# Seven written-out passes of a fused attention kernel turned into a hardware loop

## The chip, the cores and the metric

The kernel runs on one core of a Trainium2 chip. The metric is the device time of one execution in microseconds (us). TensorE multiplies matrices, VectorE (DVE), ScalarE (ACT) and GpSimd (POOL) do the elementwise work, and SyncE (SP) starts the loads and stores. Each engine has a sequencer that reads the engine's instructions one after another.

## The reference

Four blocks run one after another on `x` of shape (32, 128, 128): 32 sequences of 128 tokens with 128 features. Cut down:

```
x = L0(x, ctx, mask)    # self-attention and cross-attention, 16 heads of 64, each with
                        # a residual and a layer norm; then a ReLU MLP 128-512-128, the same
x = L1(x, ctx, skip)    # attention, 16 heads of 8, ReLU on q, k, v; + x
x = L2(x, ctx)          # an encoder layer on ctx + ctx, then a decoder layer with two
                        # linear attentions (elu + 1), 8 heads of 16, layer norms, ReLU MLPs
r = x + mha(norm(x), norm(ctx))                 # L3: 8 heads of 16
U = (norm(r) @ W_in.T + b_in) @ Bmat            # (32, 128, 64)
s_t = silu(s_(t-1) @ A.T) + U_t                 # 128 steps in order
out = r + states @ Cmat + mod                   # mod: one row for each sequence
```

Everything is float32, except for the masks inside the kernel. All but the recurrence over `t` treats the 32 sequences apart from one another.

## The kernel before

The 32 sequences go in 8 groups of 4 (`GROUPS`, `G`), so a tile has 128 partitions and 4 x 128 = 512 columns. The work on a group falls into two streams. The main stream is L0. The side stream is L1, L2 and L3 up to `U`. A pass `g` does the main stream of group `g` together with the side stream of group `g - 1`. So the kernel has these stages: pass 0 (main stream of group 0 with the setup of the weights), passes 1 to 7 (main and side), the side stream of group 7 alone, the scan over 128 steps, and the final sum with the stores.

Each compute engine has its own program for the two streams, as Python generators `main(i)` and `side(i)`, and `interleave` merges them step by step by the list `SIDE_PACE`; the order of each engine's instructions is thus fixed when the program is built. `main_fills` and `side_fills` give the order in which PSUM banks are filled, and who empties them (A for ScalarE, D for VectorE). The engines go in step by semaphores that only count up: `filled` by TensorE, `emptied` by ScalarE and VectorE, and some twenty more. A wait names the value that its semaphore must have reached, and that value is worked out from the pass: `Pass.at(each, n)` gives `g * each + n`, where `each` is how often the semaphore is raised in one pass and `n` the place in it.

All eight passes are Python loops over `g`, so their instructions are written out eight times with constant wait values. The scan and the final sum at the end are different: there `Fori`, a hardware loop with a counter in a register on each engine, holds the steps (16 scan steps in each round), with wait values and some addresses worked out from the counter.

At the end of a pass ("seam" below) TensorE turns the last normalised tile, VectorE empties it into `xT["b"]` and hands over to the side stream in `hand_over` (L1255, L1256, L1258: `x_side`, `c_side` and the mask `attend`, then `handed` goes up). The program of TensorE ends a pass with a wait for that emptying:

```python
elif kind == "n":
    before_filling(i, item, (tag, "y"))
    turn4(MAIN, item, lambda b: main_normed[:, b, :])
    if tag == "ln3":
        wait_emptied(pe, i, MAIN, item)
```

The next pass begins on TensorE with the turn of `x_in` (L642) and the side stream's products (L646), on VectorE with the masks (L1189 to L1195). SyncE has its own Python loop over the groups and starts the loads of group `g` when pass `g - 1` has read its inputs.

Of the kernel before, what the change touches and what calls it, by code (L numbers as in the profile page):

```python
# [32 lines left out]
GROUPS = B // G  # L33
# [61 lines left out]
SIDE_STEPS = len(SIDE_PACE)  # L95
SETUP_STEPS = 9


class Stream:


    def __init__(self, fills):
        self.order = [name for name, _, _ in fills]
        self.fill = {name: n + 1 for n, name in enumerate(self.order)}
        self.bank = {name: bank for name, bank, _ in fills}
        self.by = {name: by for name, _, by in fills}
        self.total = {"A": 0, "D": 0}
        self.rank = {}
        for name, _, by in fills:
            self.total[by] += 1  # L110
            self.rank[name] = self.total[by]
        self.fills = len(fills)

        self.before, last = {}, {}
        for name, bank, _ in fills:
            self.before[name] = last.get(bank)
            last[bank] = name


def main_fills():  # L120

    order, n = [], 0
    for item in (x for step in MAIN_STEPS for x in step if x[1] not in NO_FILL):
        tag, kind = item[:2]
        if kind == "s":
            bank = item[2] % 2
        elif kind == "o":
            bank = 3
        elif kind == "y":
            bank = 0  # L130
        elif item[:3] == ("ca", "v", 1) and item[3] < 2:
            bank = (1, 3)[item[3]]
        else:
            bank, n = (2, 4)[n % 2], n + 1
        if kind in ("v", "y", "n"):
            by = "D"
        elif kind in ("k", "o") or tag in ("ffn", "in"):
            by = "AD"[item[-1] % 2]
        else:
            by = "A"  # L140
        order.append((item, bank, by))
    return order
# [34 lines left out]
MAIN, SIDE = Stream(main_fills()), Stream(side_fills())  # L177
# [43 lines left out]
class Pass:  # L221


    def __init__(self, g):
        self.g = g

    def at(self, each, n):
        return self.g * each + n


def interleave(main, side, pace=SIDE_PACE):

    taken, due = 0, 0
    for n, _ in enumerate(main):
        while side is not None and taken < len(pace) and due * len(MAIN_STEPS) < (n + 1) * sum(pace):
            next(side)
            due += pace[taken]
            taken += 1
    assert side is None or next(side, "end") == "end"


def alone(stream):

    return sum(1 for _ in stream)


def build_program(nc, I, out):
    with ExitStack() as ctx:
# [149 lines left out]
        def wait_filled(eng, i, st, name):  # L398

            eng.wait_ge(filled[st], i.at(st.fills, st.fill[name]))  # L400

        def wait_emptied(eng, i, st, name):

            by = st.by[name]
            eng.wait_ge(emptied[st, by], i.at(st.total[by], st.rank[name]))
# [16 lines left out]

        def passes(eng, main, side, setup):

            interleave(main(Pass(0)), setup, [1] * SETUP_STEPS)
            for g in range(1, GROUPS):
                interleave(main(Pass(g)), side(Pass(g - 1)))
            assert alone(side(Pass(GROUPS - 1))) == SIDE_STEPS

        n_first, n_ca, n_rest, n_const = [0], [0], [0], [0]  # L430

# [2 lines left out]
        def _(sp):  # L434
# [4 lines left out]
            def load_inputs(g):  # L439
                for dst, name in ((x_in, "x"), (c_in, "ctx_1024")):  # L440
                    sp.dma_start(dst[:, :, :], I[name][g * G:g * G + G, :, :].rearrange("g t e -> t g e")).then_inc(group_in, 16)

            def load_valid(g):
                m = I["mask_BxS2_bf1"].rearrange("b t -> (b t)")[g * GT:g * GT + GT].partition_broadcast(128)
                sp.dma_start(valid_in[:, :], m).then_inc(group_in, 16)

            def load_skip(g):
                m = I["mask_BxS_ik0"].rearrange("b t -> (b t)")[g * GT:g * GT + GT].partition_broadcast(128)
                sp.dma_start(skip_in[:, :], m).then_inc(skip_loaded, 16)
# [27 lines left out]
            load_skip(0)  # L477
            for g in range(1, GROUPS):

                wait_filled(sp, Pass(g - 1), MAIN, ("in", 1))  # L480
                load_inputs(g)
                sp.wait_ge(masks_taken, g)
                load_valid(g)
                sp.wait_ge(handed, g)
                load_skip(g)
# [9 lines left out]
        def _(pool):  # L495
# [61 lines left out]
            def side(i):  # L557
# [69 lines left out]
                yield  # L627

            passes(pool, main, side, None)


        @block.tensor
        def _(pe):
# [61 lines left out]
            def turn(i, item):  # L695
                tag, _, u = item
                before_filling(i, item)
                pe.wait_ge(scaled, i.at(2 * UNITS, u + 1 + (0 if tag == "sa" else UNITS)))
                for h in range(4):
                    last = nc.tensor.transpose(bank(MAIN, item)[:, h * 128:h * 128 + 128],  # L700
                                               probs[:, u % 3, h * 128:h * 128 + 128], ident[:, :])
                last.then_inc(filled[MAIN], 1)
# [202 lines left out]
            def setup_side():  # L905
# [19 lines left out]
                yield  # L925

            passes(pe, main, side, setup_side())


# [33 lines left out]
        def _(act):  # L963
# [62 lines left out]
            def side(i):  # L1026
# [44 lines left out]
                yield  # L1071

            passes(act, main, side, None)

            def scan_step(t, k):
# [13 lines left out]
        def _(dve):  # L1089
            V = nc.vector  # L1090
            count = {setup_step: 0, main_step: 0, side_step: 0}
            each = {setup_step: SETUP_VSTEPS, main_step: MAIN_VSTEPS, side_step: SIDE_VSTEPS}

            def link(i, s, ins):

                count[s] += 1
                ins.then_inc(s, 1)
                dve.wait_ge(s, i.at(each[s], count[s]))

            once = Pass(0)  # L1100
            dve.wait_ge(consts_ready, n_const[0])
            link(once, setup_step, V.tensor_copy(ident_h[:, :], ident[:, :]))
            link(once, setup_step, V.tensor_copy(causal[:, :], main_normed[:, 0, :]))
# [148 lines left out]
            def hand_over(i):  # L1252

                wait_emptied(dve, i, MAIN, ("ln3", "n"))
                V.tensor_scalar(x_side[:, :], xT["b"][:, :], 1.0, None, ALU.mult)  # L1255
                V.tensor_scalar(c_side[:, :], cT[:, :], 1.0, None, ALU.mult)  # L1256
                dve.wait_ge(skip_loaded, i.at(16, 16))
                V.tensor_scalar(attend[:, :], skip_in[:, :], 0.0, D1 ** -0.5, ALU.not_equal, ALU.mult).then_inc(handed, 1)  # L1258
# [25 lines left out]
            def side(i):  # L1284
# [85 lines left out]
                yield  # L1370

                def group(n):
                    return slice(i.g * n, i.g * n + n)
                link(i, side_step, V.tensor_tensor(x2_all[:, group(GT)].rearrange("p (g t) -> p g t", g=G),
                                                   x1T[:, :].rearrange("p (g t) -> p g t", g=G),
                                                   mod[:, group(G)].unsqueeze(2).broadcast_to([128, G, T]), ALU.add))
# [6 lines left out]

            interleave(main(once), setup_side(), [1] * SETUP_STEPS)
            hand_over(once)
            for g in range(1, GROUPS):
                interleave(main(Pass(g)), side(Pass(g - 1)))
                hand_over(Pass(g))
            assert alone(side(Pass(GROUPS - 1))) == SIDE_STEPS

            dve.wait_ge(emptied[SIDE, "D"], GROUPS * SIDE.total["D"])

# [41 lines left out]
```

## Time and profile before

| | |
|---|---|
| median of 3 runs | 2718.73 us (2716.09 to 2722.7) |
| the profiled execution | 2722.7 us, span 2721.0 us |
| instructions recorded | 32500 |
| passes 1 to 7 (239.4 to 2306.0 us) | 2066.6 us |
| mean granted clock of TensorE | 0.903 |
| instruction fetch | two queues, 1.43 MB and 0.54 MB |

Times come from one execution by the hardware profiler, except for the first line. "Busy" counts neither waits nor the register, branch and semaphore instructions of the sequencers. The granted clock of TensorE is 1.00 at 2.4 GHz and 0.50 at 1.2 GHz. In a row of the timeline the bracket at the end is how long the engine had stood idle before it, and whose work released it. A pass is read here from one hand-over (L1255) to the next.

### The profile page before, as it was taken

What the parts mean: (1) busy time and instruction counts of PE and PEld (TensorE: products, weight loads), DVE (VectorE), ACT (ScalarE), POOL (GpSimd) and SP (SyncE); (2) the same over time, 40 slices, a digit from 0 to 9 for tenths busy, and PEclk for the clock granted to TensorE, in tenths of its full rate; (3) what the DMA queues carried; (4) which work ended last, traced back from release to release, by engine and by line L of the source; (5) the groups of instructions that cost most, each with busy time, mean ns of one, the idle gap of its engine ahead of it and who ended that gap; (6) DMA issues with size and microseconds to landing.
All of it is one profiled execution on the core that took longest, in us unless ns stands there. A gap on an engine that the chain in (4) does not pass through costs nothing.

```text
span 2721.0 us, 32500 instructions
## 1 busy us (share of the span) xinstructions
PE 2321.0 (85%) x11161; PEld 1613.0 (59%) x11161; DVE 1502.9 (55%) x3998; ACT 1168.8 (43%) x4001; POOL 340.7 (13%) x349
## 2 busy tenths in 40 slices
PE   5887988898888988898889888998889888865898
PEld 3555655666565665565556656566556555543596
DVE  4554666565756666566656674666656665233212
ACT  3452635364544645363536454454536353210221
POOL 0002011101112011201110111101120121012000
PEclk9988999999999999999999998999999999566555
DMA  5000000000000000000000000000000000000001
GB/s 152 1 1 13 1 1 1 13 2 1 1 1 13 1 1 1 13 1 1 1 13 1 1 1 1 13 1 1 1 5 1 1 1 1 0 0 0 1 0 31
DMA packets 24511, 19.75 MB, mean 7 GB/s; under 512 B 1699, under 2 KB 22182, under 8 KB 24358
## 3 DMA queue, kind: packets, MB, share of 16 engines
q1 hardware_dynamic: 24358, 17.78, 2.3%
q8 instruction: 87, 1.43, 0.2%
q14 instruction: 66, 0.54, 0.1%
HBM read 15.68 MB, written 2.10 MB: 7 GB/s over the span
## 4 chain that ended last, share of the span: by engine, by line
PE 65%; DVE 21%; ACT 7%; issue 4%; POOL 3%; SPq 0%; DMA 0%; POOLq 0%; DVEq 0%
PE ps L646 13%; PE ps L654 8%; PE ps L787 7%; PE ps L689 7%; PE ps L712 6%; PE ps L770 4%; PE ps L780 4%; DVE tok L1158 3%; PE ps L700 3%; ACT probs L977 3%; DVE keys L1225 2%; PE ps L939 2%; PE ps L642 2%; DVE stats L1145 2%; POOL kx L563 2%
## 5 line engine op out<-in xcount | busy, mean ns | idle before, releaser
L977 ACT ACTIVATE probs<-ps,neg_max 128x128 f32<-128x128 f32 x1024 | 361.8, 366 | 419.4 <-DVE neg_max L1138 412.6
L977 ACT ACTIVATE s_probs<-ps,s_max 128x128 f32<-128x128 f32 x768 | 218.8, 367 | 274.0 <-DVE s_max L1138 273.9
L689 PE MATMUL ps<-keys,queries 128*128 128x256 f32 x1024 | 281.3, 398 | 28.4 <-ACT queries L971 28.4
L712 PE MATMUL ps<-probsT,values 128*128 128x256 f32 x1024 | 277.8, 395 | 3.7 <-ACT headsT L1011 2.7
L787 PE MATMUL ps<-kx,qT 32*128 32x512 f32 (+1 forms) x384 | 244.5, 720 | 33.5 <-POOL kx L563 33.5
L1138 DVE TENSOR_REDUCE neg_max<-ps 128x4 f32<-128x512 f32 x256 | 176.4, 689 | 162.7 <-PE ps L692 161.4
L1138 DVE TENSOR_REDUCE s_max<-ps 128x4 f32<-128x512 f32 x192 | 132.5, 690 | 235.7 <-PE ps L787 233.5
L689 PEld LDWEIGHTS ps<-keys,queries 128*128 128x128 f32 x1024 | 187.4, 195 | 119.6 <-ACT queries L971 42.4
L540 POOL TENSOR_TENSOR rstd<-var_eps,minus_half 128x4 f32<-128x4 f32 x88 | 90.3, 1026 | 1235.3 <-DVE var_eps L1151 1234.6
L1145 DVE BATCH_NORM_STATS2 stats<-ps 128x6 f32<-128x128 f32 x352 | 78.2, 284 | 299.4 <-PE ps L654 295.6
L712 PEld LDWEIGHTS ps<-probsT,values 128*128 128x128 f32 x1024 | 178.8, 194 | 67.3 <-issue 25.1
L977 ACT ACTIVATION_READ_ACCUMULATOR probs<-ps,neg_max 128x1 f32 x1024 | 208.7, 204 | 0.0
L700 PEld LDWEIGHTS ps<-ident,probs 128*128 128x128 f32 x1024 | 123.5, 142 | 128.2 <-issue 81.9
L971 ACT ACTIVATE probsT<-ps 128x512 f32<-128x512 f32 x256 | 155.7, 608 | 50.7 <-PE ps L700 49.5
L770 PEld LDWEIGHTS ps<-l1v,s_probsT 128*128 128x128 f32 x1024 | 143.9, 209 | 51.9 <-issue 49.3
L700 PE MATMUL ps<-ident,probs 128*128 128x128 f32 x1024 | 158.6, 278 | 0.4 <-DVE probs L1181 0.4
L642 PE MATMUL ps<-ident,tok 128*128 128x128 f32 x352 | 61.6, 302 | 103.8 <-DVE tok L1158 89.6
L646 PE MATMUL ps<-xT_a,w_qkv_sa 128*128 128x512 f32 x256 | 132.1, 603 | 12.8 <-DVE cT L1210 11.0
L780 PE MATMUL ps<-ident,s_probs 128*128 128x128 f32 x768 | 133.0, 300 | 10.3 <-ACT s_probs L977 7.3
L534 POOL TENSOR_TENSOR pool_scratch<-minus_half 128x1 f32<-128x1 f32 x88 | 17.0, 193 | 985.0 <-DVE x1T L1275 672.1
L770 PE MATMUL ps<-l1v,s_probsT 128*128 128x9 f32 x1024 | 137.1, 261 | 0.7 <-ACT s_probsT L971 0.7
L1240 DVE COPY headsT<-ps 64x256 f32<-64x256 f32 x256 | 107.5, 420 | 40.3 <-PE ps L712 38.2
(211 smaller groups left out, 4088.9 us busy)
## 6 DMA issues: line engine op xcount, KB each, us to landing
x_in<-in_x SPq DMA_DIRECT2D x8, 256.0 KB, 3.0
c_in<-in_ctx SPq DMA_DIRECT2D x8, 256.0 KB, 3.3
skip_in<-in_mask_BxS_ik SPq DMA_DIRECT2D x8, 256.0 KB, 3.1
out<-x_all SPq DMA_DIRECT2D x8, 256.0 KB, 2.3
valid_in<-in_mask_BxS_bf SPq DMA_DIRECT2D x8, 64.0 KB, 3.4
w_qkv_sa<-in_L_xattn_sa_wq SPq DMA_DIRECT2D x1, 512.0 KB
w_qkv_sa<-in_L_xattn_sa_wk SPq DMA_DIRECT2D x1, 512.0 KB
w_qkv_sa<-in_L_xattn_sa_wv SPq DMA_DIRECT2D x1, 512.0 KB
```

The lines of the kernel that those rows point to most:

```text
L646: mm(bank(st, name)[0:lhs.shape[-1], :], lhs, rhs, start=True, stop=True).then_inc(filled[st], 1)
L654: last = mm(dst, l, r, start=(n == 0), stop=(n == len(todo) - 1))
L689: mm(bank(MAIN, item)[:, n * 256:n * 256 + 256], queries[:, c % 2, at], keys[:, c % 2, :, at], start=(n == 0), stop=False, skip_group_chec ...
L700: last = nc.tensor.transpose(bank(MAIN, item)[:, h * 128:h * 128 + 128], probs[:, u % 3, h * 128:h * 128 + 128], ident[:, :])
L712: last = mm(bank(MAIN, item)[:, n * 256:n * 256 + 256], values[:, c // 4, b0 + n, (c % 4) * 128:(c % 4) * 128 + 128], probsT[:, u % 2, n * ...
L770: last = mm(bank(SIDE, (tag, "o", b))[:, at:at + d1], s_probsT[:, u % 2, h * 128:h * 128 + 128], value[:, b, q * 4 + h, :], start=True, st ...
L780: last = nc.tensor.transpose(bank(SIDE, (tag, "t", u))[:, h * 128:h * 128 + 128], s_probs[:, u % 2, h * 128:h * 128 + 128], ident[:, :])
L787: mm(bank(SIDE, (tag, "s", s)), qT[part, b * T:b * T + T], kx[part, :, b * T:b * T + T], start=True, stop=True).then_inc(filled[SIDE], 1)
L971: A(dst, view(s) if view else s, fn, **kw).then_inc(emptied[st, "A"], 1)
L977: last = A(dst[:, u % dst.shape[1], h * 128:h * 128 + 128], bank(st, (tag, "s", u))[:, h * 128:h * 128 + 128], ACT.Exp, bias=src_max[:, u ...
L1138: V.tensor_reduce(dst[:, u % 2, :], bank(st, (tag, "s", u)).rearrange("p (h k) -> p h k", h=4), AX.X, ALU.max, negate=True).then_inc(max_r ...
L1145: last = V.bn_stats(stats[:, slot, b, :], bank(st, (tag, "y"))[:, b * 128:b * 128 + 128])
```

## The change

The passes 1 to 7 become one hardware loop of 7 rounds on TensorE, ScalarE, VectorE and GpSimd. `Pass` now holds an optional register `r` and a constant offset: in a round, the main stream is `Pass(r, 1)` and the side stream `Pass(r, 0)`, and a wait value is `r * each + (offset * each + n)`. Pass 0 and the last side stream keep constants. On VectorE `hand_over` is in the loop, and two instructions at the end of the side stream take their addresses in `x2_all`, `mod` and `u_all` from the register (`bass.ds`). SyncE keeps its written-out list.

```diff
-    def __init__(self, g):
-        self.g = g
+    def __init__(self, r, offset):
+        self.r, self.offset = r, offset
 
     def at(self, each, n):
-        return self.g * each + n
+        known = self.offset * each + n
+        return known if self.r is None else self.r * each + known
...
-            interleave(main(Pass(0)), setup, [1] * SETUP_STEPS)
-            for g in range(1, GROUPS):
-                interleave(main(Pass(g)), side(Pass(g - 1)))
-            assert alone(side(Pass(GROUPS - 1))) == SIDE_STEPS
+            interleave(main(Pass(None, 0)), setup, [1] * SETUP_STEPS)
+            with eng.Fori(0, GROUPS - 1) as r:
+                interleave(main(Pass(r, 1)), side(Pass(r, 0)))
+            assert alone(side(Pass(None, GROUPS - 1))) == SIDE_STEPS
...
-                wait_filled(sp, Pass(g - 1), MAIN, ("in", 1))
+                wait_filled(sp, Pass(None, g - 1), MAIN, ("in", 1))
...
                 def group(n):
-                    return slice(i.g * n, i.g * n + n)
+                    return slice(i.offset * n, i.offset * n + n) if i.r is None else bass.ds(i.r * n + i.offset * n, n)
...
-            for g in range(1, GROUPS):
-                interleave(main(Pass(g)), side(Pass(g - 1)))
-                hand_over(Pass(g))
-            assert alone(side(Pass(GROUPS - 1))) == SIDE_STEPS
+            with dve.Fori(0, GROUPS - 1) as r:
+                interleave(main(Pass(r, 1)), side(Pass(r, 0)))
+                hand_over(Pass(r, 1))
+            assert alone(side(Pass(None, GROUPS - 1))) == SIDE_STEPS
```

## Rows read from the trace of the kernel before

**Rows 1.** The page: busy time by engine; granted clock in 40 slices.
```profile
PE 2321.0 (85%) x11161; PEld 1613.0 (59%) x11161; DVE 1502.9 (55%) x3998; ACT 1168.8 (43%) x4001; POOL 340.7 (13%) x349
...
PEclk9988999999999999999999998999999999566555
```

**Rows 2.** Windows by stage: stretch, length, busy by engine (instructions), PEclk, DMA, GB/s.
```profile
239.40:2306.00 2066.60, 1814.13 (x9212) 1247.50 (x9212) 1277.89 (x3353) 998.10 (x3388) 293.96 (x287) 0.97 0.01 3
2306.00:2572.00 266.00, 192.42 (x592) 120.59 (x592) 79.28 (x234) 48.69 (x130) 33.70 (x32) 0.57 0.00 0
```

**Rows 3.** Windows of single passes, the longest and the shortest, same columns.
```profile
534.40:831.50 297.10, 261.37 (x1317) 179.24 (x1317) 182.42 (x480) 142.58 (x484) 41.89 (x41) 0.96 0.01 4
...
1125.00:1418.50 293.50, 257.29 (x1316) 177.25 (x1316) 182.74 (x479) 142.59 (x484) 42.13 (x41) 0.98 0.01 4
```

**Rows 4.** The page: chain that ended last, by engine.
```profile
PE 65%; DVE 21%; ACT 7%; issue 4%; POOL 3%; SPq 0%; DMA 0%; POOLq 0%; DVEq 0%
```

**Rows 5.** Timeline at one seam: start, us, engine, line, op, operands, count, idle before.
```profile
1122.84 0.63 PE L642 MATMUL ps<-ident,main_normed 128*128 128x128 f32 x4 [1.47 <-DVE main_normed L1158]
1123.33 1.00 DVE L1377 TENSOR_SCALAR u_all<-ps 64x512 f32<-64x512 f32 x1
1124.19 0.77 DVE L1171 TENSOR_SCALAR xT_b<-ps,col_all 128x512 f32<-128x512 f32 x1
...
1125.02 0.66 PE L642 MATMUL ps<-ident,x_in 128*128 128x128 f32 x4 [1.55 <-DVE xT_b L1171]
...
1125.68 0.42 DVE L1258 TENSOR_SCALAR qT<-skip_in 128x512 f32<-128x512 int32 x1
1125.71 0.60 ACT L971 ACTIVATE xT_a<-ps 128x512 f32<-128x512 f32 x1 [5.47 <-PE ps L642]
...
1126.15 1.12 PE L646 MATMUL ps<-x_side,turned 128*128 128x512 f32 x2 [0.47 <-DVE qT L1258]
```

**Rows 6.** Windows of 3.4 us at that seam.
```profile
1120.40:1123.80 3.40, 1.60 (x6) 0.51 (x6) 2.43 (x6) 0.00 (x0) 0.90 (x1) 1.00 0.00 0
1123.80:1127.20 3.40, 1.71 (x7) 0.99 (x8) 3.30 (x8) 0.60 (x1) 0.81 (x2) 0.99 0.01 4
1127.20:1130.60 3.40, 3.40 (x12) 2.37 (x11) 2.53 (x5) 0.69 (x1) 3.40 (x4) 0.50 0.21 73
```

**Rows 7.** DMA view: instruction queue (packets, MB, share); loads, KB each, us to landing.
```profile
q8 instruction: 87, 1.43, 0.2%
...
valid_in<-in_mask_BxS_bf SPq DMA_DIRECT2D x8, 64.0 KB, 3.4
...
kx<-in_L_xattn_W_prog SPq DMA_DIRECT2D x1, 32.0 KB, 1.9
```

**Rows 8.** Waits of TensorE: total us, times, longest.
```profile
PE ps L689 <- ACT queries L971: 28.4, 32, 2.5
```

**Rows 9.** Timeline of the scan, ScalarE, then VectorE.
```profile
2573.49 0.19 ACT L1079 ACTIVATE state<-ps 64x32 f32<-64x32 f32 x1 [2.56 <-PE ps L935]
...
2586.28 0.19 ACT L1079 ACTIVATE state<-ps 64x32 f32<-64x32 f32 x1 [0.72 <-PE ps L939]
2587.28 0.19 ACT L1079 ACTIVATE state<-ps 64x32 f32<-64x32 f32 x1 [0.81 <-PE ps L939]
2588.27 0.19 ACT L1079 ACTIVATE state<-ps 64x32 f32<-64x32 f32 x1 [0.80 <-PE ps L939]
2589.18 0.19 ACT L1079 ACTIVATE state<-ps 64x32 f32<-64x32 f32 x1 [0.72 <-PE ps L939]
...
2602.08 0.19 ACT L1079 ACTIVATE state<-ps 64x32 f32<-64x32 f32 x1 [0.83 <-PE ps L939]
...
2586.28 0.18 DVE L1397 TENSOR_TENSOR u_all<-u_all,state 64x32 f32<-64x32 f32 x1 [0.73 <-PE ps L939]
...
2589.29 0.18 DVE L1397 TENSOR_TENSOR u_all<-u_all,state 64x32 f32 x1 [0.80 <-PE ps L939]
```

**Rows 10.** The page: the turn of `probs` on TensorE; last columns are idle before.
```profile
L700 PE MATMUL ps<-ident,probs 128*128 128x128 f32 x1024 | 158.6, 278 | 0.4 <-DVE probs L1181 0.4
```

More of the change, by code:

```diff
@@ L1098, in link @@
                 dve.wait_ge(s, i.at(each[s], count[s]))
-            once = Pass(0)
+            once = Pass(None, 0)
             dve.wait_ge(consts_ready, n_const[0])
```

## The prediction

> **What bounds the kernel now.** I read the page first. One core is busy 85% of the span on TensorE, 55% on VectorE, 43% on ScalarE and 13% on GpSimd [rows 1]; no engine is full, so the order of the work decides. Next, the stages: passes 1 to 7 take 2066.6 of 2721.0 us, and the last side stream alone 266.0 [rows 2]. The change acts on passes 1 to 7 only. Pass by pass they take 293.5 to 297.1 us, and the longer ones have the lower mean granted clock, 0.96 against 0.98 [rows 3]. The chain of waits is 65% TensorE, 21% VectorE, 7% ScalarE and 4% "issue" [rows 4]: within a pass the queue of TensorE sets the pace, with short stops for VectorE and ScalarE. Then I read one seam between two passes in time [rows 5]. TensorE turns `main_normed` at 1122.84, VectorE empties that bank by 1124.96, and at 1125.02 TensorE turns `x_in` for the next pass. VectorE meanwhile hands over until 1126.10, and TensorE starts the side stream's first product at 1126.15. So TensorE is already thinly used here, and the clock is granted at half for the 3.4 us that follow [rows 6].
>
> **The change, part by part.** The work, its tiles, semaphores, counts and order stay. What goes is the written-out code of six of the seven middle passes on TensorE, ScalarE, VectorE and GpSimd. What comes is (a) a jump back after each of the first six rounds, (b) arithmetic for every wait value inside the round, since `Pass.at` now holds a register, and (c) register addresses for two VectorE instructions per pass. SyncE keeps its written-out list, so loads and their order do not move. Pass 0 and the side stream after the loop keep constant waits.
>
> (a) **The jump.** A loop is already in this kernel: the scan, 7 rounds of 16 steps. Written-out steps follow one another in 0.913 us (2573.49 to 2586.28 is 14 steps), so 16 of them would take 14.62; a round takes 14.80 (2587.28 to 2602.08) [rows 9]. Jump and register work together cost 0.2 us per round. That body is short. The body here is long: instruction fetches come in packets of 16 KB on one queue, 87 packets in the execution [rows 7], which is 1.43 MB, over ten packets for each of the eight passes. I take it that such a body is no longer at hand when the jump asks for its head, and that the first packet has to be fetched while the engine stands. The trace of before has no such stop. From below it is 0.2 us (the scan's round); from above it is a transfer that nobody prepared. Loads take 1.9 us from issue to landing for 32 KB and 3.4 us for the 64 KB of `valid_in` [rows 7]. I take 3.0 us, near the upper of these rows because a sequencer that has run dry also has to ask for the packet, and 0.2 for the jump itself: 3.2 us.
>
> Whom does it stop? TensorE's last act in a pass is to wait for VectorE's emptying of `("ln3","n")`; the jump stands behind that wait, so its fetch begins at about 1125.0 and nothing of TensorE's covers it. Of that time TensorE would in any case stand 0.47 us before 1126.15, waiting for the hand-over [rows 5], so 3.2 - 0.5 = 2.7 us are exposed. ScalarE has nothing to do for the 5.47 us before 1125.71 [rows 5], so its own fetch is covered. VectorE's sequencer is ahead of its engine: with waits riding on queued instructions it reaches the jump about when `u_all` begins (1123.3) and has its packet by about 1126.5, 0.4 us after the hand-over ends; its masks are then 0.4 us late, under TensorE's 2.7. GpSimd has 41 instructions in a pass [rows 3] and waits most of it. So the four jumps overlap and TensorE's counts: 6 x 2.7 = 16 us. If TensorE's fetch were covered too, the term would be 6 x 0.2 = 1 us; if VectorE's whole 3.2 stood behind them, 6 x 5.9 = 35 us.
>
> The Trainium skill, "Runtime: NRT & Kernel Launch", section "Instruction fetch mechanics", says that fetching is sequential and mostly hidden, and that a taken branch to a target outside the fetched window stalls for the fetch, which would make the term the 16 us above and not 1; the rows of before neither show nor exclude that stall. The skill's "Advanced Engine Details and Errata", section "Control Flow Timing", gives 108 ns for a compare-and-branch; six of them would be an estimate of 0.6 us, against 0.2 us per round in the scan, which holds register work as well.
>
> **The clock.** At the seam TensorE is busy 1.60 and 1.71 of 3.4 us in two stretches and then gets the half clock for one such stretch, 1127.2 to 1130.6 [rows 6]. With 2.7 more idle microseconds I expect the low stretch to be one stretch longer. The price of low clock comes from rows 3: 297.1 us at 0.96 against 293.5 at 0.98 is 3.6 us for a low share greater by 4 points of 295, or 12 us: 0.3 us per us. One stretch costs 3.4 x 0.3 = 1.0 us; at most, with TensorE never waiting, 1.7. Six: 6 us, between 0 and 10.
>
> (b) **Register waits.** Per pass the code has some 366 waits on TensorE, 312 on VectorE, 168 on ScalarE and 26 on GpSimd (counted in the program). Each value now takes an addition by the sequencer. In the scan the same forms cost nothing in 14 of 16 steps: ScalarE starts 0.72 us after its release in both kinds of code. In the first two steps of a round it starts 0.81 and 0.80 after [rows 9]; there the addition for a second wait carries the first wait, so that the sequencer stands where before the queued instruction stood. That is 0.09 us per such stop. On VectorE the step with a register address starts at 2589.29 where ScalarE's starts at 2589.18, 0.11 us later, while both start at 2586.28 in written-out code. TensorE has some 118 places per pass with two waits or more. Written out, the second wait was an instruction of its own and the first rode on the work; in the loop this turns round. Where the last release is the first wait of the code, the place loses 0.09 us; where it is the second, it gains. TensorE stood 32 times for `queries` in the execution, 4 times in a pass [rows 8], at `scores`, where the first wait is the one released last: 4 x 0.09 x 7 = 2.5 us, which I round to 3; the other places I take as even. Elsewhere the additions run ahead of the array, which is busy 0.6 to 1 us per group while an addition is a matter of the sequencer alone. If that cover is gone, all 118 lose: 118 x 7 x 0.09 = 74 us. If all gain, it is -74.
>
> (c) **Register addresses.** Two VectorE instructions per pass, late by 0.11 us each, at the end of the side stream: 1.5 us over seven, of which I count none. The bound is 1.5, since they stand right ahead of VectorE's last work at the seam.
>
> **Sum** against the profiled execution: 2722.7 us (span 2721.0), plus 16 (jumps), 6 (clock), 3 (waits): 2747.7. The median of the runs shown is 2718.7, 4.0 below that execution, so I predict 2744 us, 0.9% more.
>
> **Rivals.**
> - **Cheap jump.** The head of the body is there when wanted, as in the scan, or the fetch is covered by the seam's idle time. Then 6 x 0.2 + 3 = 4 us: 2722, within measuring error. For it: TensorE idles 1.8 of its 3.4 us at the seam already, and the scan. Against: a body of ten packets, and a last wait that holds TensorE's jump until 1125.0, after which only 0.47 us of its time is free.
> - **Dear waits.** The additions hold the TensorE sequencer in many places, and it loses its lead over the array. 40 to 74 us on top of the jumps: about 2780 to 2815. For it: 118 double waits in a pass and "issue" already 4% of the chain. Against: 14 of 16 steps of the scan.
> - **Turned waits gain (the other sign).** Most TensorE stops come from the wait that now rides on the work itself. It is faster than before by more than 0.2% only if more than 25 + 5.4 = 30 us are won, over 340 of the 826 places at 0.09 us, or with cheap jumps over 70 net. At two thirds of the places net: 2744 - 3 - 50 = 2691. Against: the clearest place of that kind, the turn of `probs` with `scaled` as its second wait, held the array idle for 0.4 us in the whole execution [rows 10].
>
> **How the numbers follow.** Forecast 0.68; its own range is 2731 (fetch 1.9 us, so 1.6 exposed, and no clock term: 10 + 3 us over the median) to 2767 (35 + 10 + 3 us over it). Cheap jump 0.14. Dear waits 0.12. Turned waits 0.06. About 0.2%, 5.4 us, is what a measurement of this kernel can tell from no change. Cheap jump gives 0.12 same and 0.02 slower: faster 0.06, same 0.12, slower 0.82. The range 2721 to 2785 leaves out the gaining case, most of the dear waits and a sliver of the cheap jumps, just under 0.2 together.
>
> **What the profile after would show.** Passes 2 to 7, each entered by a jump, are 3 to 5 us longer; pass 1, entered by falling through, is not, and neither are the side stream alone, the scan or pass 0. The gap before TensorE's turn of `x_in` grows from 1.5 to about 4.7 us at six seams, with the releaser no longer VectorE's; the half clock behind it lasts about 6.8 us. Busy times stay. If instead all seven passes are longer, by gaps spread over the attention, it is the waits. If no seam widens, the jump is cheap. What would make me wrong: a fetch of several microseconds that also repeats inside the body, a stall on VectorE that outlasts TensorE's, or clock stretches elsewhere in the pass that shift by chance.

## The result, and the profile after

The changed kernel takes 2753.4 us (median of 4 runs, 2748.5 to 2757.3) against 2717.5 for the kernel before: a ratio of 1.0129, 95% interval 1.011 to 1.0148, or 36 us more. The forecast was 2744 us, 25 more than the 2718.7 known then. The profiled execution took 2753.06 us, its span is 2751.3. Some executions of these kernels run slower throughout at a lower granted clock, and every ratio here leaves them out.

The page of the changed kernel, busy time and granted clock:

```profile
PE 2333.3 (85%) x11161; PEld 1616.3 (59%) x11161; DVE 1504.4 (55%) x3998; ACT 1170.6 (43%) x4001; POOL 340.6 (12%) x349
...
PEclk9998999999999999999999999999999999566555
```

The counts of [rows 1] have not changed. TensorE is busy 12 us longer on the same 11161 products, at a mean granted clock of 0.895 in place of 0.903; VectorE and ScalarE are busy less than 2 us longer. Below are the windows of single passes (stretch, length, busy time of each engine with its instructions, granted clock, DMA share, GB/s). A pass runs from one handing over of `x_side` to the next, and the first shown is pass 1:

```profile
241.91:537.49 295.58, 260.87 (x1316) 179.06 (x1316) 182.31 (x480) 142.87 (x484) 41.96 (x41) 0.96 0.01 4
537.49:837.37 299.88, 259.73 (x1316) 177.87 (x1316) 182.85 (x479) 142.85 (x484) 41.96 (x41) 0.96 0.01 4
...
1137.84:1438.20 300.36, 261.47 (x1316) 179.48 (x1316) 182.81 (x480) 142.74 (x484) 41.95 (x41) 0.95 0.01 4
...
2038.94:2339.34 300.40, 261.42 (x1316) 179.54 (x1316) 182.82 (x480) 142.73 (x484) 41.96 (x41) 0.95 0.01 2
```

Pass 1, entered by falling through, is 0.6 us longer than in the first trace of before; the six passes entered by a jump are 2.8 to 6.9 us longer than the same passes there, 30.2 in sum. The two spans differ by 30.3: the passes behind a jump account for it. Pass 0 is 2.5 us longer and the part behind pass 7 is 3.0 us shorter, which nearly cancel. Against passes of 293.5 us [rows 3] each of them is 6.4 to 7.0 us longer.

One seam in time (start, us, engine, line, operation, operands, idle before and what ended it). It answers to [rows 5]:

```profile
1437.39 0.77 DVE L1172 TENSOR_SCALAR xT_b<-ps,col_all 128x512 f32<-128x512 f32 x1
1438.20 0.43 DVE L1256 TENSOR_SCALAR x_side<-xT_b 128x512 f32<-128x512 f32 x1
...
1441.61 0.43 DVE L1190 TENSOR_SCALAR mask_ca<-valid_in 128x512 bf16<-128x512 uint8 x1 [2.31 <-issue]
...
1442.51 1.11 PE L643 MATMUL ps<-ident,x_in 128*128 128x128 f32 x4 [6.08 <-issue]
...
1443.42 1.92 PE L647 MATMUL ps<-x_side,turned 128*128 128x512 f32 x2
```

VectorE has emptied `xT_b` at 1438.16. Before, TensorE turned `x_in` 0.06 us later; now 4.35 us later, and the releaser is no longer VectorE but "issue". This is the longest of the six: counted from the start of the hand-over, the turn comes 3.75 to 4.31 us later, 4.0 in the mean, where it was 0.02. The view of waits has this stop six times, once a seam; below it is the wait at `scores` that answers to [rows 8]:

```profile
PE ps L643 <- issue: 34.7, 6, 6.1
...
PE ps L690 <- ACT queries L972: 29.3, 32, 2.3
```

The second has grown by 0.9 us in all. The first is not spread over the loop's code: one instruction has it, the branch. Six of them take 3.40 to 3.96 us; the seventh, at 76 ns, falls out of the loop. The view of the loop's line, TensorE's sequencer (count, then min/median/max in ns):

```profile
L427 PEldq COMPARE_BRANCH  x7: 76/3618/3958, 537.7 to 2339.5; - x7
```

The queue of instruction packets, in the DMA view, against 87 packets and 1.43 MB in [rows 7] (the second such queue goes from 0.54 to 0.93 MB):

```profile
q8 instruction: 108, 1.77, 0.3%
```

VectorE's `mask_ca` is 2.31 us late too, by its own jump, but that ends ahead of TensorE's. Last, the clock. Rows of 3.4 us at the seam before that one, against one such row at half clock in [rows 6], and then six further rows of the same pass, the first of them at full clock:

```profile
1136.70:1140.10 3.40, 0.00 (x0) 0.00 (x0) 2.21 (x5) 0.00 (x0) 0.00 (x0) 0.50 0.05 14
1140.10:1143.50 3.40, 1.91 (x6) 1.40 (x7) 2.39 (x5) 0.60 (x1) 0.08 (x1) 0.50 0.23 77
1143.50:1146.90 3.40, 3.40 (x9) 1.85 (x8) 0.92 (x2) 0.69 (x1) 3.40 (x5) 0.50 0.00 0
1259.60:1263.00 3.40, 1.38 (x7) 0.86 (x8) 3.35 (x9) 0.00 (x0) 0.18 (x1) 1.00 0.01 2
1263.00:1266.40 3.40, 3.40 (x9) 1.85 (x8) 0.80 (x2) 1.19 (x2) 1.74 (x2) 0.50 0.00 0
1283.50:1286.90 3.40, 3.40 (x8) 1.80 (x8) 1.80 (x3) 0.00 (x0) 1.68 (x2) 0.51 0.00 0
1355.10:1358.50 3.40, 3.16 (x10) 2.04 (x10) 2.75 (x6) 2.98 (x11) 0.00 (x0) 0.50 0.02 5
1368.80:1372.20 3.40, 3.40 (x9) 2.28 (x8) 0.55 (x2) 1.77 (x6) 0.00 (x0) 0.50 0.00 0
1420.00:1423.40 3.40, 3.14 (x7) 1.32 (x5) 2.52 (x11) 0.48 (x1) 2.46 (x3) 0.50 0.00 0
```

In this pass the granted clock is half (1.2 of 2.4 GHz) for 27.3 us, eight rows' worth, and 10.2 us of that lie together at the seam. A pass of 293.5 us of the first trace has 13.7 us, four rows' worth. Passes 2 to 7 have 18.0 us in the mean in the first trace of before and 25.8 here.

### The profile page after: what moved, and what is told of

It is laid out like the page before. It is cut to its first block, busy times and chain, and to the rows that moved or that the text cites. A ratio compares the mean times of both kernels' runs of the same rounds, so it can differ in the third digit from the quotient of the medians.

```text
span 2751.3 us, 37417 instructions
## 1 busy us (share of the span) xinstructions
PE 2333.3 (85%) x11161; PEld 1616.3 (59%) x11161; DVE 1504.4 (55%) x3998; ACT 1170.6 (43%) x4001; POOL 340.6 (12%) x349
## 4 chain that ended last, share of the span: by engine, by line
issue 69%; PE 13%; POOL 11%; DVE 4%; ACT 2%; SPq 0%; POOLq 0%; DMA 0%; DVEq 0%
POOL kx L564 4%; POOL rstd L541 3%; PE ps L940 2%; PE ps L647 2%; PE ps L936 2%; POOL s_probsT L569 2%; POOL main_residual L554 1%; PE ps L788 1%; PE ps L655 1%; ACT probs L978 1%; PE ps L690 1%; ACT s_probs L978 1%; PE ps L781 1%; PE ps L953 1%; POOL pool_scratch L535 1%
## 5 line engine op out<-in xcount | busy, mean ns | idle before, releaser
L535 POOL TENSOR_TENSOR pool_scratch<-minus_half 128x1 f32<-128x1 f32 x88 | 17.1, 195 | 1015.2 <-DVE x1T L1276 670.9
```

## The experiments

Each ratio is against the kernel before on the same chip. Its median was 2709.4 us next to the first four kernels below (registers, the two split loops, two passes to a round), 2710.4 next to the hint, the moved wait, the pause of eight copies and the lighter seam, and 2714.2 next to the last four (the pause of two copies, before again, registers on TensorE, hint with lighter seam).

**Registers without a jump.** The kernel before, written out; on all four engines every wait value and address of the middle passes comes from a register that holds 0.

```diff
+            zero = nc.alloc_registers("base", engines=[eng.engine])
+            nc.regs_mov(zero, 0)
+            r = nc.snap(zero, min_val=0, max_val=1)
             for g in range(1, GROUPS):
-                interleave(main(Pass(g)), side(Pass(g - 1)))
+                interleave(main(Pass(r, g)), side(Pass(r, g - 1)))
```

> The seven passes are written out as before, but every wait value and the two VectorE addresses are worked out from a register that holds 0, as in the loop: the arithmetic without the jump. Theory (the jump stops TensorE at six seams, and the rest is small): 0 to +5 us over before, as pass 1 of the changed kernel, entered without a jump, is only 0.6 us longer than before (295.6 against 295.0). Rival (dear waits): +20 to +36 us, the whole of the change's cost, and the passes grow by gaps inside the attention.

Measured 2725.8 us, ratio 1.006 (1.0043 to 1.0076): 16 us, not 0 to 5. The gaps in the attention have not grown. The weight loads of the turn of `probs`, whose second wait is `scaled`, on the page of this kernel:

```profile
L704 PEld LDWEIGHTS ps<-ident,probs 128*128 128x128 f32 x1024 | 125.3, 144 | 128.3 <-issue 122.2
```

Its idle time is 128.3 us; in before the same group of weight loads has 128.2, with another releaser named for a part of it. Its execution in the trace is the fastest of its six, 2722.5 us. Three of its passes are as short as before's shortest (windows, the first and a long one):

```profile
537.55:831.06 293.51, 257.39 (x1316) 176.97 (x1316) 182.69 (x480) 142.87 (x484) 42.15 (x41) 0.98 0.01 4
...
1124.33:1421.23 296.90, 261.67 (x1316) 179.50 (x1316) 182.78 (x480) 142.74 (x484) 41.96 (x41) 0.96 0.01 4
```

So the registers don't lengthen a pass evenly; they make more passes long. What has grown is the gap at the seam (timeline, hand-over at 1421.23):

```profile
1419.56 1.00 DVE L1381 TENSOR_SCALAR u_all<-ps 64x512 f32 x1 [0.21 <-DVE x_all L1378]
...
1421.41 1.11 PE L646 MATMUL ps<-ident,x_in 128*128 128x128 f32 x4 [1.96 <-DVE xT_b L1175]
```

TensorE stands 1.96 us ahead of `x_in` at each of these six seams, in place of 1.55. VectorE's instruction with a register address waits 0.21 us right ahead of the emptying, and the turn itself starts 0.18 us after the hand-over begins in place of 0.02.

The chain on the page of the changed kernel has 69% "issue" against 4% in [rows 4]. Here, with no jump and 16 us lost, it has 66%, so that share does not measure what the jump costs.

**Only TensorE loops; all but TensorE loop; two passes to a round.** In the first, ScalarE, VectorE and GpSimd are written out with constants, in the second TensorE is; the third has three rounds of two passes and pass 7 written out, so two jumps in place of six. The upper part of the diff is of the first (only TensorE's stream has a `setup` here; the second turns the condition round), the lower of the third.

```diff
+            if setup is not None:
+                with eng.Fori(0, GROUPS - 1) as r:
+                    interleave(main(Pass(r, 1)), side(Pass(r, 0)))
+            else:
+                for g in range(1, GROUPS):
+                    interleave(main(Pass(None, g)), side(Pass(None, g - 1)))
...
+            with eng.Fori(0, 3) as q:
+                for n in range(2):
+                    interleave(main(Pass(q * 2, n + 1)), side(Pass(q * 2, n)))
+            interleave(main(Pass(None, 7)), side(Pass(None, 6)))
```

> TensorE alone loops; ScalarE, VectorE and GpSimd have written-out passes with constants. Theory: nearly the whole cost, +28 to +36 us over before, since TensorE's branch takes 3.4 to 4.0 us at each of six seams and the half clock behind it lasts 10.2 us instead of 3.4. Rival (the stops of several engines add up): clearly less, +10 to +22 us, with the rest in the run without TensorE's loop.

> ScalarE, VectorE and GpSimd loop as in the changed kernel; TensorE's seven passes are written out with constants. Theory (TensorE's jump counts, the other engines' jumps lie under it): TensorE's 4.4 us stop at six seams goes; what is left is VectorE's jump, which in the changed kernel ends 2.3 us after its hand-over, so +1 to +2.5 us for each of six seams plus a little clock: +6 to +18 us over before. Rival (VectorE's jump sets the seam just as well, both stand side by side): +25 to +36 us. Rival (only TensorE's jump costs): 0 to +4 us.

> Three rounds of two passes each, pass 7 written out: two jumps instead of six, register values in six passes instead of seven. Theory (5.0 us for each jump): 2 x 5 = 10 us over before, +8 to +14 with the waits' small share; of the passes only those entered by a jump (the third and the fifth) grow. Rival (dear waits): about as slow as the changed kernel, +28 us or more. Rival (a long body costs more as it gets longer, by fetches inside it): the passes not entered by a jump grow too.

TensorE alone: 2746.9 us, ratio 1.0135 (1.0117 to 1.0152), as much as the whole change. The other three alone: 2731.5, ratio 1.0075 (1.0059 to 1.0091), 22 us where 6 to 18 were expected, and 6 above the registers alone. Two jumps: 2736.4, ratio 1.0094 (1.0076 to 1.0111), 27 us where 8 to 14 were expected: that one missed, by about what the registers cost. With the other engines' loop the passes have one length (windows; the other five behind a jump lie between 296.96 and 297.11):

```profile
829.38:1126.36 296.98, 260.15 (x1316) 177.79 (x1316) 183.50 (x480) 142.57 (x484) 42.08 (x41) 0.97 0.01 4
```

At its seam TensorE goes on at once, and VectorE's stop of 2.01 us lies under its work (timeline, hand-over at 1126.36):

```profile
1126.38 1.12 PE L647 MATMUL ps<-ident,x_in 128*128 128x128 f32 x4 [1.73 <-DVE xT_b L1176]
...
1129.47 0.75 DVE L1194 TENSOR_SCALAR mask_ca<-valid_in 128x512 bf16<-128x512 uint8 x1 [2.01 <-issue]
```

In the kernel with two jumps, exactly the two passes behind a jump are at 300.4 us:

```profile
827.04:1127.41 300.37, 261.49 (x1316) 179.42 (x1316) 183.14 (x480) 142.74 (x484) 41.95 (x41) 0.95 0.01 4
1127.41:1424.38 296.97, 261.69 (x1316) 179.47 (x1316) 182.78 (x479) 142.73 (x484) 41.96 (x41) 0.96 0.01 4
1424.38:1724.78 300.40, 261.38 (x1316) 179.55 (x1316) 182.80 (x479) 142.72 (x484) 41.99 (x41) 0.95 0.01 4
```

**The jump with a hint.** The changed kernel, each engine's stream told of the jump's target at the head of the round.

```diff
-            with eng.Fori(0, GROUPS - 1) as r:
+            with nc.Fori(0, GROUPS - 1, engines=[eng.engine], hint_back_edge=True) as r:
```

> The changed kernel with the loop's back edge hinted to each engine (its instruction stream carries a hint of the jump's target ahead of the jump). Theory: the stop of 3.4 to 4.0 us at TensorE's six jumps is the fetch of the loop's head, so a hint that works takes the recorded branch to under 1 us, x_in's turn comes about 1.5 us after the hand-over's start again, the half clock behind a seam falls back from 10.2 towards 3.4 us, and what is left is the registers' share: 2709 + 16 = about 2725 us, a ratio of 1.004 to 1.008. Rival: the stop is a cost of the jump itself, or the hint comes too late to fetch anything, and nothing changes: ratio 1.011 to 1.015, branches still at 3.4 to 4.0 us.

Measured 2730.0 us, ratio 1.0075 (1.0062 to 1.0088). The loop's line on TensorE:

```profile
L427 PEldq BRANCH_PREFETCH_HINT  x7: 31/40/45, 239.3 to 2018.9; - x7
...
L427 PEldq COMPARE_BRANCH  x7: 80/436/476, 533.6 to 2317.7; - x7
```

Its turn of `x_in` in a pass whose hand-over began at 1129.66 (timeline):

```profile
1130.60 1.11 PE L643 MATMUL ps<-ident,x_in 128*128 128x128 f32 x4 [2.71 <-DVE xT_b L1172]
```

The branch falls from 3.6 to 0.44 us, so the stop was the fetch of the loop's head and not a cost of jumping. VectorE's stop ahead of `mask_ca` is gone too, so that was its own fetch. `x_in` is turned 0.9 us after the hand-over begins in the mean of six seams, in place of 4.0. Of the 3.1 us won at a seam 3.0 show in the passes: behind pass 2 (296.8 us) they alternate between 299.3 to 299.4 and 294.6 to 294.7 us, and passes 2 to 7 are 297.4 us in the mean, against 300.3.

**The wait behind the jump.** The changed kernel; TensorE's wait for `("ln3","n")` stands at the start of the next pass, behind the jump.

```diff
+                if i.offset:
+                    wait_emptied(pe, Pass(i.r, i.offset - 1), MAIN, ("ln3", "n"))
...
-                            if tag == "ln3":
-                                wait_emptied(pe, i, MAIN, item)
```

> The changed kernel with TensorE's wait for the emptying of xT_b moved from ahead of the jump to behind it, so that the jump can begin when TensorE's last turns are issued (1436.5 in the changed kernel's trace) and not when VectorE has emptied them (1438.2). Theory: 1.7 us of each fetch then lie under VectorE's work; x_in's turn comes 4.35 - 1.7 = 2.6 us after the emptying, and the time falls by 6 x 1.7 = 10 us or a little more by the clock: ratio 1.007 to 1.0105. Rival: the pass is set by VectorE's own jump (its mask_ca comes at 1441.6), then nothing is gained: 1.011 to 1.015.

Measured 2732.9 us, ratio 1.0077 (1.0064 to 1.009). The jump began earlier, though by 0.7 and not 1.7 us: TensorE's branch starts 0.54 us ahead of the hand-over in place of 0.19 behind it, and still takes 3.6 us. `x_in` is turned 3.44 us after the hand-over begins in the mean, in place of 4.0 (below, 1433.86 against 1430.55). The first three passes behind a jump are uneven (302.2, 298.5, 300.0 us), the last three equal and 3.4 us shorter than the 300.4 of the changed kernel. One turn of `x_in` (timeline) and the last pass (windows):

```profile
1433.86 1.11 PE L643 MATMUL ps<-ident,x_in 128*128 128x128 f32 x4 [5.08 <-issue]
```

```profile
2024.48:2321.43 296.95, 258.56 (x1316) 178.01 (x1316) 182.94 (x480) 142.44 (x484) 41.90 (x41) 0.97 0.01 2
```

**A pause and no loop.** The kernel before, written out with constants; at six seams TensorE waits for idle copies of ScalarE. Eight copies, then two.

```diff
+            if eng.engine == nc.scalar.engine:
+                wait_emptied(eng, Pass(g), MAIN, ("ln3", "n"))
+                for k in range(PAUSE):
+                    nc.scalar.activation(idle[:, 1, :], idle[:, 0, :], ACT.Copy).then_inc(paused, 1)
+                    eng.wait_ge(paused, PAUSE * (g - 1) + k + 1)
+            elif eng.engine == nc.tensor.engine:
+                eng.wait_ge(paused, PAUSE * g)
```

> The kernel before, written out, no loop and no register; at the six seams TensorE waits until ScalarE has done eight 128x256 copies of some 0.5 us each after the emptying of xT_b: x_in's turn comes about 4.1 to 4.5 us after the emptying in place of 0.06 us behind the start of the hand-over, as long as the stop in the changed kernel. Theory: an idle TensorE costs the same whatever it idles for, and the seam's loss is the stop of 2.9 us net plus a longer stretch at half clock (10 us in place of 3.4): the six passes come to 299 to 301 us, +28 us, ratio 1.009 to 1.012. Rival A: the clock has no part, only the stop counts: 6 x 2.9 = 17 us, ratio 1.005 to 1.008. Rival B: in the changed kernel half of the excess is not TensorE's stop at all but the other engines' jumps: then the pause costs under 12 us, ratio below 1.005.

> The kernel before, written out, with the pause of two copies in place of eight: TensorE is held about 1.0 us at each of six seams (eight copies: 1.015). Theory: the loss comes in steps, since a pass ends at 293.5, 297.0 or 300.4 us by how many pieces at half clock fall in it: 1.0 us is enough to take most passes from 293.5 to 297.0, and the ratio is 1.005 to 1.009, several times the 6 us (1.002) that were held. Rival: the loss grows with the pause, 6 x 1.0 to 1.3 us: ratio 1.002 to 1.004.

Eight copies: 2749.8 us, ratio 1.015 (1.0135 to 1.0165), above the range of the theory and far above both rivals. The timeline, hand-over at 1130.92:

```profile
1130.92 3.55 ACT L439 ACTIVATE idle<-idle 128x256 f32<-128x256 f32 x8 [4.76 <-DVE xT_b L1186]
...
1134.73 1.09 PE L656 MATMUL ps<-ident,x_in 128*128 128x128 f32 x4 [5.34 <-ACT idle L439]
```

Three passes in a row (windows):

```profile
1130.92:1429.20 298.28, 258.64 (x1316) 178.08 (x1316) 182.56 (x480) 146.20 (x493) 41.97 (x41) 0.97 0.01 4
1429.20:1729.71 300.51, 260.93 (x1316) 179.32 (x1316) 182.54 (x480) 146.19 (x493) 41.96 (x41) 0.96 0.01 4
1729.71:2032.03 302.32, 262.69 (x1316) 180.68 (x1316) 182.55 (x479) 146.16 (x492) 41.96 (x41) 0.95 0.01 4
```

The three sum to 901.1 us, 300.4 each in the mean, with TensorE held 3.8 us. So a TensorE that merely waits costs as much as one that fetches (39 us here, 36 for the change); neither registers nor jump are needed for a mean pass of 300.4 us. Two copies: 2730.5 us, ratio 1.0057 (1.0045 to 1.007). Two eighths of 3.8 us are about 1.0 of holding; at six seams that is 6 us, and it cost 16. No trace shows how its passes divide.

**A lighter seam.** The kernel before, written out; ScalarE empties the side stream's `u` in place of VectorE, and the addition into `x_all` comes earlier.

```diff
-               (("l3", "z"), 6, "A"), (("l3", "u"), 7, "D")]
+               (("l3", "z"), 6, "A"), (("l3", "u"), 7, "A")]
```

> The kernel before, written out, with two pieces of VectorE's work taken off the seam: the side stream's u is emptied by ScalarE and the addition into x_all comes earlier in the side stream. In the trace of before they take 1.0 and 0.68 us right ahead of xT_b's emptying. Theory: what delays VectorE at the seam is paid in full, by TensorE's stop and then by the clock; 7 x 1.7 = 12 us less, ratio 0.994 to 0.998. Rival: the stop only moves (the turned residual, or the norm of the pass's last layer is what ends last, and ScalarE's emptying comes later than VectorE's did): ratio 0.999 to 1.002.

Measured 2709.4 us, ratio 0.9997 (0.9988 to 1.0005): no gain, against the theory. TensorE stands 0.91 us ahead of `x_in` in place of 1.55, and the pass is not shorter. The half clock behind the seam is gone, and 3.4 us of it appear 119 us behind the hand-over instead, where before had full clock: 13.7 us in both (timeline; windows):

```profile
1114.70 0.66 PE L642 MATMUL ps<-ident,x_in 128*128 128x128 f32 x4 [0.91 <-DVE xT_b L1174]
```

```profile
1114.68:1408.22 293.54, 257.12 (x1316) 177.01 (x1316) 181.94 (x479) 143.62 (x485) 42.12 (x41) 0.98 0.01 4
```

**The kernel before again, and registers on TensorE alone.** The second is the first experiment with the register on TensorE only.

```diff
+            r = None
+            if eng.engine == nc.tensor.engine:
+                zero = nc.alloc_registers("base", engines=[eng.engine])
...
```

> The kernel before, unchanged, for a second trace and for what the comparison makes of no change. The kernel with the lighter seam (2709 us, as before) has all seven passes at 293.5 to 294.1 us in its trace, while the one trace of before has four of seven above 294.6. Theory: a pass takes 293.5 us where only three pieces at half clock of 3.4 us fall in it and up to 297.1 where six or seven do, and before's usual execution on this chip is one with nearly all passes at 293.5, so this trace has a mean pass of 293.5 to 294.5 and a span near 2705 to 2709; the 2721.0 of the first trace was of another chip and above its usual. Rival: before's passes lie at a mean of 295 here too, and the lighter seam did gain in its passes what it lost elsewhere. Ratio 0.999 to 1.001 by both.

> The kernel before, written out, with waits from a register of value 0 on TensorE alone (1,449 instructions more, as with TensorE's loop alone); no jump. Theory: what the registers cost comes through TensorE, which has the short waits on the path; the ratio is most of the 1.006 of all engines' registers: 1.004 to 1.007. Rival A: the cost comes by the other engines' longer waits (VectorE's and ScalarE's chains of short operations, as where they alone loop, 1.0075): then 0.999 to 1.002 here. Rival B: the cost is split, 1.002 to 1.004.

Before against itself: ratio 0.9996 (0.9982 to 1.0009), span 2707.6 us. One pass of 297.1, then five of 293.5 in a row. (In the first trace five of seven passes are above 294.6 us, not four.) Windows:

```profile
531.19:828.32 297.13, 261.32 (x1316) 179.28 (x1316) 182.58 (x479) 142.87 (x484) 41.95 (x41) 0.96 0.01 4
828.32:1121.86 293.54, 257.23 (x1316) 177.21 (x1316) 182.87 (x479) 142.87 (x484) 42.19 (x41) 0.98 0.01 4
```

Its pass from 1121.86 has four rows' worth at half clock. And at 1239.90 it comes to the same gap as the changed kernel at 1259.60:

```profile
1124.00:1127.40 3.40, 3.40 (x12) 2.37 (x11) 2.60 (x5) 0.69 (x1) 3.40 (x4) 0.50 0.22 74
...
1239.90:1243.30 3.40, 1.50 (x8) 0.97 (x9) 3.33 (x9) 0.00 (x0) 0.10 (x1) 1.00 0.00 0
1243.30:1246.70 3.40, 3.40 (x17) 2.17 (x16) 0.71 (x2) 2.12 (x4) 1.74 (x2) 1.00 0.00 0
1342.40:1345.80 3.40, 2.50 (x3) 0.99 (x4) 0.40 (x1) 0.00 (x0) 0.84 (x1) 0.50 0.02 5
1345.80:1349.20 3.40, 3.40 (x9) 2.50 (x8) 0.30 (x1) 1.90 (x6) 0.00 (x0) 0.50 0.00 0
1397.10:1400.50 3.40, 3.26 (x10) 1.89 (x9) 2.54 (x11) 0.00 (x0) 1.79 (x3) 0.51 0.00 0
```

TensorE is busy 1.50 us there and 1.38 in the changed kernel, on the same instructions; here full clock follows, there half. Registers on TensorE alone: 2720.1 us, ratio 1.0026 (1.0011 to 1.0042), the range of the split. That the rest comes by the other engines is not shown by it, since costs here do not add (below). In its trace TensorE stands 1.78 us ahead of `x_in`, and the passes are 293.8, 293.4 and then four of 296.96 to 296.98 us.

**Hint and lighter seam together.**

```diff
+            with nc.Fori(0, GROUPS - 1, engines=[eng.engine], hint_back_edge=True) as r:
...
+               (("l3", "z"), 6, "A"), (("l3", "u"), 7, "A")]
```

> The changed kernel with both: the hinted back edge on all four engines and the lighter seam (u emptied by ScalarE, the addition into x_all earlier). The hinted loop alone is at 1.0075, the lighter seam alone at 0.9997 with 1.7 us more room at each seam. Theory: the loss of the hinted loop is that the seam comes a little too late and each pass then takes on further pieces at half clock; 1.7 us of room give it back, and the loop costs what the registers cost within a pass: 1.000 to 1.004. Rival: room at the seam is worth nothing here either, as it was worth nothing in the kernel written out: 1.006 to 1.009.

Measured 2711.7 us, ratio 0.9983 (0.9972 to 0.9994): better than the theory had it, and the best ratio of the study, though 0.17% is at the edge of what can be told. The gap ahead of `x_in` is 1.8 us, against 2.7 with the hint alone. Seven passes of 293.5 to 293.6 us, registers, jumps and all (windows, the first and the last):

```profile
239.52:533.15 293.63, 258.74 (x1316) 177.76 (x1316) 182.01 (x479) 143.47 (x485) 41.90 (x41) 0.97 0.01 4
...
2000.97:2294.51 293.54, 258.54 (x1316) 178.00 (x1316) 181.82 (x478) 143.48 (x485) 41.89 (x41) 0.97 0.01 2
```

Its 12 runs lie between 2709.2 and 2715.8 us; the 29 of before next to them reach from 2707.2 to 2723.2.

## Why the prediction was right, and where it was not

**The mechanism held.** TensorE's jump finds its target not at hand and fetches it while the engine stands: the branch takes 3.6 us, one told of its target ahead 0.44. This is the stall that the Trainium skill, "Runtime: NRT & Kernel Launch", section "Instruction fetch mechanics", describes for a taken branch out of the fetched window; the trace agrees, with 3.2 us as the difference. The jumps of the other engines lie under it: TensorE alone costs 1.0135, all four 1.0129. The seam, pass 1 and the unchanged work came out as foretold, but VectorE's own fetch did not: its masks were to be 0.4 us late, and they are 2.0 to 2.3 us late, which still ends ahead of TensorE's stop. The cheap jump is excluded by the branch itself, the dear waits and the gaining waits by the idle time of the turn of `probs` (128.2 and 128.3 us) and by passes of 293.5 us with registers throughout.

**The jump, (a), was sized too small.** I took 3.2 us for fetch and jump, 2.7 exposed. The branch begins 0.19 us after the hand-over does, takes 3.6, and the turn of `x_in` follows 0.2 later: 4.0 us in the mean of six seams, before 0.02. Less the 0.47 that TensorE used to wait behind that turn, 3.5 us are exposed: 6 x 3.5 = 21, not 16.

**The rest was too small as well, by how much depends on what it is held against.** I forecast 9 us for clock and waits. Between the two profiled executions passes 2 to 7 grow by 30.2 us, of which 21 are the stop: 9 are left. That it is the same 9 is luck, since neither part of it came where and as large as forecast. But that execution of before was among its slower ones. I allowed for it by taking 4.0 us off, and the changed kernel's execution was at its median, so nothing was to be taken off there. Between the medians 36 - 21 = 15 us are left, and against passes of 293.5 us, 6 x (300.3 - 293.5) - 21 = 20. These remainders are differences; no run splits them into clock and registers. Half clock was to last one row of 3.4 us longer per seam. It lasts 7.7 us longer per pass than in the first trace, and only a part of that lies at the seam. The price of 0.3 us for each us of half clock came from clocks of two digits: the two passes of [rows 3] have 22.8 and 13.7 us of it, which makes 0.4. Over these passes it is 9 / 46 = 0.2, and two kernels with passes of 293.54 us have 13.7 and 17.1 us of half clock, so there is no fixed price. The prediction named half clock that shifts elsewhere in the pass as what would make it wrong; it did shift, and the forecast still held with 2753 in a range of 2731 to 2767. The pause shows that a standing TensorE is enough for the whole loss.

**The register waits, (b), have a cost, but not the one I worked out.** The 3 us were to come from stops of 0.09 us at `scores`, where 0.9 us were found. Alone, the registers cost 16 us (1.006), while the shortest passes stay at 293.5; they raise how many passes are long. The register address of (c), which I counted at nothing, is a part of it: 0.21 us right ahead of the last emptying. On top of TensorE's loop (jump and registers) the other engines' loops add nothing that can be seen; no run has TensorE's jump without register waits. Two terms that I summed do not add: registers 16, two jumps 27, six on TensorE 37, all of it 36.

**What joins them: pass lengths come in steps.** In the traces, passes that repeat do so at 293.54 us (before, the lighter seam, the hinted loop with the lighter seam), at 296.96 (all but TensorE looping, the wait behind the jump, registers on TensorE, the hinted loop as a mean over two) or at 300.4 (the change, the two passes behind a jump where there are two, the pause as a mean over three). The steps are 3.4 us. Kernels whose stops ahead of `x_in` differ by 0.9 us (the lighter seam, and with the hint) have the same length to 0.02 us, and less than 1 us at a seam moved a pass by 3.4 or by nothing. The wait behind the jump took three passes from 300.4 to 296.95 for 0.6 us. The lighter seam gave nothing where most passes were at 293.5 already and, from the hinted loop at 1.0075 to 0.9983, 25 us for 0.9 us at each of six seams. Two copies of pause cost 16 us for 6. The registers fit in. The stop ahead of `x_in` is 1.55 us in both traces of before, and two and one of their passes 2 to 7 take 297 us. It is 1.73 us with all but TensorE looping, 1.78 with registers on TensorE and 1.96 with registers on all engines, and six, four and three of these passes take 297 us. So 0.2 us at the seam may be enough. No run changed that stop by 0.2 us alone, and the counts do not rise with it, so this is argued.

That the steps exist is shown. Why is argued: the same gap in TensorE's work is followed by half clock in one pass and not in another, by where it lies against the moments at which the clock changes, and a pass keeps its length once each next one meets them alike. In the second trace of before the clock falls at about 2.1, 220.5 and 275.2 us behind the hand-over in all five passes of 293.5 us, which agrees. No run moved these moments alone, so this stays open.

## What to carry to other kernels

A jump back over a long body cost TensorE 3.6 us here with nothing under it; a hint at the head of the loop took it to 0.44 us, and a wait that could stand behind the jump gained there (1.0129 to 1.0077). Where a kernel repeats a pass with a gap in TensorE's work, price a delay at the gap not by its own length but by the step that the pass may take, here 3.4 us or nothing, and look at the lengths of single passes before believing a ratio of half a per cent. A loop with the hint and a little room at its seam ran as fast as the code written out.

## What the runs showed that I had not expected

- VectorE's branch is recorded with 0.06 us, and still its first instruction behind the jump is 2.0 to 2.3 us late, with "issue" as its releaser, and not late with the hint (3.2 us late with two passes to a round): on that engine the fetch does not show in the branch.
- The hinted branch still takes 0.44 us on TensorE, and `x_in` comes 0.9 us after the hand-over begins where registers alone make it 0.18.
- Pass 0, whose code and place did not change, ended between 233.0 us (the pause) and 242.0 us (registers on all engines) in the traces that are read above, with no relation to the edit that I can see.
